# Moving the routing of an expert layer into the experts' block of a two-layer transformer kernel

## The reference

```python
scores = sigmoid(x @ w_gate.T)                          # [T, 16]
sv = scores.reshape(T, 4, 4)                            # 4 groups of 4 experts
group_scores = top_k(sv, 2)[0].sum(-1)
top_groups = top_k(group_scores, 2)[1]                  # 2 of 4 groups allowed
masked = where(allowed[:, :, None], sv, -inf).reshape(T, 16)
_, idx = top_k(masked, 4)                               # 4 experts of those
w = take_along_axis(scores, idx, 1); w = w / (w.sum(-1) + 1e-06)
combine = (one_hot(idx, 16) * w[..., None]).sum(1)      # [T, 16]
g = silu(einsum('th,efh->tef', x, w1_e)); u = einsum('th,efh->tef', x, w3_e)
routed = einsum('tef,ehf,te->th', g * u, w2_e, combine)
out = x + routed + swiglu(x, w1_s, w3_s, w2_s)
```

## Time and profile before

| | |
|---|---|
| median of 3 runs | 2229.55 us (2228.36, 2229.55, 2238.91) |
| the profiled execution | 2230.54 us, of which the span of the trace is 2228.7 us |
| TensorE busy | 1991.5 us, 89% of the span |
| VectorE busy | 1618.8 us, 73% |
| ScalarE busy | 1343.3 us, 60% |
| GpSimd busy | 1107.5 us, 50% |
| granted TensorE clock, mean | 0.95 of full |

### The profile page before, as it was taken

The page is one execution under the profiler, slowest core; times in us unless marked ns, Lnnn a source line. Parts: engine busy times, 40 slices in busy tenths (PEclk is TensorE's granted clock), DMA queues, the critical chain, the costliest instruction groups (busy, mean ns, idle before and its releaser), DMA issues. The chain is left out here.

```text
span 2228.7 us, 56143 instructions
## 1 busy us (share of the span) xinstructions
PE 1991.5 (89%) x17787; PEld 1012.5 (45%) x17787; DVE 1618.8 (73%) x3426; ACT 1343.3 (60%) x2148; POOL 1107.5 (50%) x994
## 2 busy tenths in 40 slices
PE   4788999999999999995599979999999999999775
PEld 3534444444444444445244424444444444444444
DVE  4977888888888888866677766566656666667896
ACT  2245666666666666663355547777877777778421
POOL 1432322222233222234254538777877778778565
PEclk7779999999999999997799979999999999999897
DMA  5621222112222211100012341111111111110000
GB/s 132 187 54 47 54 53 51 50 50 51 53 53 53 53 51 50 50 24 1 1 48 75 110 127 29 44 29 29 43 29 29 43 29 29 43 29 2 0 15 24
DMA packets 127064, 107.24 MB, mean 48 GB/s; under 512 B 39636, under 2 KB 102724, under 8 KB 126956
## 3 DMA queue, kind: packets, MB, share of 16 engines
q1 hardware_dynamic: 120544, 99.83, 16.9%
q10 hardware_dynamic: 6412, 6.18, 1.0%
HBM read 76.01 MB, written 29.53 MB: 47 GB/s over the span
## 5 line engine op out<-in xcount | busy, mean ns | idle before, releaser
L1103 DVE TENSOR_REDUCE b_mx<-psum 128x1 f32<-128x512 f32 x1024 | 664.0, 686 | 148.6 <-PE psum L920 83.4
L1087 ACT ACTIVATE b_prob<-psum 128x1024 f32<-128x1024 f32 x512 | 524.4, 1024 | 327.2 <-PE psum L952 327.1
L1917 POOL TENSOR_TENSOR combT<-attn,f_phi 128x512 f16<-128x512 f32 x512 | 587.0, 1157 | 182.0 <-ACT f_phi L2051 152.4
L2072 DVE TENSOR_REDUCE f_mx<-psum 128x1 f32<-128x512 f32 x512 | 328.6, 683 | 170.1 <-PE psum L1941 169.8
L2050 ACT ACTIVATE attn<-psum 128x512 f32<-128x512 f32 x512 | 308.0, 602 | 176.2 <-PE psum L1952 167.0
L1000 PE MATMUL psum<-b_prob,combT 128*32 128x256 f32 x4096 | 329.1, 393 | 1.5 <-ACT b_prob L1087 0.5
L852 POOL COPY combT<-v 128x64 f32 (+1 forms) x64 | 15.7, 246 | 604.4 <-PE psum L1000 594.8
L2051 ACT ACTIVATE f_phi<-psum 128x512 f16<-128x512 f32 x512 | 306.2, 598 | 0.0
L952 PE MATMUL psum<-x,b_toep 128*128 128x79 f16 (+1 forms) x4224 | 268.4, 208 | 0.0
L952 PEld LDWEIGHTS psum<-x,b_toep 128*128 128x128 f16 x4224 | 236.7, 99 | 9.3 <-issue 2.6
L855 POOL TENSOR_TENSOR x<-flip,grev 128x1024 f16<-128x1024 f16 x128 | 240.7, 1901 | 0.0
(11 more groups left out here) (321 smaller groups left out, 3391.4 us busy)
## 6 DMA issues: line engine op xcount, KB each, us to landing
f_qk<-d_qk SPq DMA_DIRECT2D x192, 128.0 KB, 2.9
d_qk<-e_qk SPq DMA_DIRECT2D x64, 256.0 KB, 2.6
b_toep<-d_line SPq DMA_DIRECT2D x128, 64.0 KB
b_q<-d_q SPq DMA_DIRECT2D x128, 54.0 KB
d_k<-a_qk SPq DMA_DIRECT2D x48, 128.0 KB, 2.3
b_toep<-d_line SPq DMA_DIRECT2D x128, 32.0 KB
b_q<-b_m SPq DMA_DIRECT2D x256, 1.0 KB
b_q<-d_q SPq DMA_DIRECT2D x128, 27.0 KB
```

The lines of the kernel that those rows point to most:

```text
L1087: nc.scalar.activation(prob[:, t % 4, :].rearrange("p (a n) -> p a n", a=2), ps[:, EXP + 2 * (t % 2):EXP + 2 * (t % 2) + 2, :], ACT.Exp).t ...
L1103: nc.vector.tensor_reduce(mx[:, b, t, half:half + 1], ps[:, bank, :], AX.X, ALU.max).then_inc(s.max_read, 1)
L1917: nc.gpsimd.tensor_tensor(plo[:, t % 4, at], prob[:, t % 4, at], phi[:, t % 4, at], ALU.subtract).then_inc(s.plo_ready, 1)
L2072: nc.vector.tensor_reduce(mx[:, b, t, half:half + 1], ps[:, bank + half, :], AX.X, ALU.max).then_inc(s.max_read, 1)
```

## The change

`phase_route` becomes `route_parts`, which has no block of its own: it hands out functions that `phase_experts` calls in its own block. Its scratch tiles lie in `g.attn` (free by then) and no longer in tiles of their own; the sizes are the same.

* VectorE: `choose` (the whole ranking for 32 tiles, and then the weights of the four tiles of chunk 0, `weigh(0, CT)`), the units 0 and 1 of chunk 0, then `weigh_rest` (the weights of the other 28 tiles), then the frames.
* TensorE: the turned weights; the GATE and UP products of units 0 and 1 without the COMB matmul; the four transposes of chunk 0 into bank 6; the two COMB matmuls; then frame 0, in which the four transposes of chunk 1 to 7 stand at the start of steps 2 to 8, all into bank 7. Frame 1 starts with a wait for the last of these to be moved.
* ScalarE: the moves of the turned weights; `silu` of unit 0; the move of chunk 0's shares; unit 1; in frame 0 the move of chunk c's shares stands ahead of unit c + 3 (for c = 6 and 7 ahead of the "next" units 0 and 1).
* GpSimd: the two clears of `g.combT`, then as before.

```diff
+    def choose(dve):
...
+        ranks(masked[:, :, :], rank[:, :, :], less16[:, :, :], cmp16, NE)
+        link(v.tensor_scalar(rank[:, :, :], rank[:, :, :], 3.5, None, ALU.is_lt))
+
+        def weigh(t0, t1):
+            sl, k = sc[:, t0:t1, :], t1 - t0
+            link(v.tensor_tensor(sl, sl, rank[:, t0:t1, :], ALU.mult))
+            link(v.tensor_reduce(total[:, t0:t1], sl, AX.X, ALU.add))
+            link(v.tensor_scalar(total[:, t0:t1], total[:, t0:t1], 1e-6, None, ALU.add))
+            link(v.reciprocal(total[:, t0:t1], total[:, t0:t1]))
+            link(v.tensor_tensor(sl, sl, total[:, t0:t1].rearrange("p (t a) -> p t a", a=1).to_broadcast([P, k, NE]), ALU.mult))
+            link(v.tensor_copy(hi16[:, t0:t1, :], sl))
+            v.tensor_copy(parts[:, t0:t1, 0:NE], hi16[:, t0:t1, :])
+            v.tensor_tensor(parts[:, t0:t1, NE:2 * NE], sl, hi16[:, t0:t1, :], ALU.subtract).then_inc(r.ready, 1)
+
+        weigh(0, CT)
+        r.weigh_rest = lambda: weigh(CT, NT)
...
+    def turn_shares(pe, c):
+
+        pe.wait_ge(r.ready, 1 if c == 0 else 2)
+        pe.wait_ge(r.moved, 1 if c == 0 else 1 + c)
+        for k in range(CT):
+            ins = nc.tensor.transpose(ps[0:2 * NE, bank_of(c), k * P:(k + 1) * P], parts[:, c * CT + k, :], g.ident[:, :])
+        ins.then_inc(r.turned, 1)
+
+    def move_shares(act, c):
+        act.wait_ge(r.turned, c + 1)
+        nc.scalar.copy(g.combT[0:2 * NE, c * CHUNK:(c + 1) * CHUNK], ps[0:2 * NE, bank_of(c), :]).then_inc(r.moved, 1)
...
+        routing.turn_weights(pe)
         for f in range(2):
-            up(0, 0, f)
+            up(0, 0, f, True)
+        routing.turn_shares(pe, 0)
+        pe.wait_ge(routing.moved, 2)
+        pe.wait_ge(routing.cleared, 2)
+        for f in range(2):
+            nc.tensor.matmul(ps[:, COMB + f, :], g.expert[:, f, :], g.combT[:, 0:CHUNK], start=True, stop=True).then_inc(s.up_psum, 1)
 
         def frame(n, u, units, ahead, out, projects, beside=None):
+            first = isinstance(n, int) and n == 0
+            if isinstance(n, int) and n == 1:
+                pe.wait_ge(routing.moved, NC + 1)
             for f in range(FT):
+                if first and 2 <= f <= NC:
+                    routing.turn_shares(pe, f - 1)
                 if f + 2 < FT and units:
                     up(n, u, f + 2)
...
-        for f in range(2):
-            unit(0, 0, f)
+        routing.move_weights(act)
+        silu(0, 0, 0)
+        routing.move_shares(act, 0)
+        unit(0, 0, 1)
 
         def frame(n, u, units, ahead, out, projects, beside=None):
             for kind, k in FRAME:
+                if isinstance(n, int) and n == 0:
+                    c = k - 3 if kind == "unit" else FT - 3 + k if kind == "next" else 0
+                    if 1 <= c < NC:
+                        routing.move_shares(act, c)
...
+        routing.choose(dve)
         for f in range(2):
             unit(0, 0, f)
+        routing.weigh_rest()
```

220 lines of the change are left out of this document (108 added, 112 removed).

## The result

The changed kernel took **2211.98 us** (median; 2208.41 to 2220.72), the kernel before 2225.78 us (2217.91 to 2270.44). Ratios leave out executions that are more than 1.5% above the fastest of their kernel; medians hold all. The ratio is 0.9941, with a 95% interval of [0.9922, 0.9961]: faster by 0.4 to 0.8%, some 13 us.

What follows compares the result with a forecast made beforehand. VectorE's ranking chain was taken to bound the path up to the first unit, TensorE from the second on. 8.9 us less 3.1 and 2.15 gave 3.65, so 2229.55 - 3.6 = 2225.9 us; range 2222 to 2231.

Steps and rivals of the forecast that it cites:

- The start: At the routing's barrier: seven `credit` increments ahead of VectorE's ranking delay it 0.5 us, bounds 0 and 0.9.
- Unit 0: First expert unit: VectorE starts it at about 1081.7 in place of 1090.56, 8.9 us earlier.
- The rest of the weights: Behind unit 1: VectorE's weights of the other 28 tiles take 3.9 us, nearly all covered by TensorE's own work.
- The clock: TensorE around frame 0's start: full clock back by 1088 or so, letting 17 matmuls end near 1089.5.
- Rival 3: Frame 0: half clock persists and makes the kernel slower, up to 18 us and 2244 us; chance 0.05.
- the late rise: Frame 0: full clock only at 1092, the 17 matmuls end at 1091.1, about 1.6 us longer, 2227.5 us.
- Waits: Frame 0: TensorE's turns wait for ScalarE's moves out of bank 7, which come in first, so no cost.
- Rival 2: Frame 0: bank 7 makes each turn wait 0.6 us, 3.6 us in all, no gain, 2229.5 us; chance 0.18.
- TensorE idle ahead of a turn: Frame 0: a gap before a chunk's transposes in the changed profile would show the forecast wrong; no size given.
- rival 1: Routing start and half clock of 1290.0 to 1293.3: more gain is kept, 2.5 us more, 2223.4 us; chance 0.12.
- The local sum: Routing through frame 0: 8.9 us won at unit 0, less 3.1 for VectorE's rest and 2.15 for transposes, 3.65 us.
- it carries to the end: Everything behind frame 0: shifts with it, so the whole 3.6 us comes off the total time.

Runs made afterwards that it cites:

- e4: Changed kernel with the split undone, all weights and all 32 transposes ahead of the first COMB matmul; ratio to the kernel before 0.9935.
- e7: Changed kernel with all of VectorE's weights ahead of unit 0, transposes still spread over frame 0; ratio to the kernel before 0.9924.
- e5: Kernel before with 252 ScalarE instructions more, waits long met, in the routing block; ratio 0.9963, second attention's loop 718.7 us.
- e6: Changed kernel with four ScalarE instructions more, waits long met, under the ranking; ratio to the kernel before 0.9971, second attention's loop 731.8 us.
- e1: Changed kernel run again with no edit; ratio to the kernel before 0.997, second attention's loop 717.8 us.
- e2: Kernel before run again as if a variant, with no edit; ratio 0.998, second attention's loop 726.8 us.
- e3: Kernel before with five TensorE instructions more, waits long met, at the routing block's end; ratio 0.9995, second attention's loop 728.5 us.
- e8: Changed kernel with 14 ScalarE instructions more, waits long met, under the ranking; ratio to the kernel before 0.9914, second attention's loop 709.8 us.
- e9: Changed kernel with the rest of VectorE's weights in three pieces, behind units 1, 3 and 5; ratio to the kernel before 0.995.
- e10: Kernel before with 10 ScalarE instructions more, waits long met, in the routing block; 2211.25 us beside 2235.44, ratio 0.9894.
- e11: Changed kernel without the split of VectorE's weights and with 14 ScalarE instructions more; ratio to the kernel before 0.9851, second attention's loop 709.3 us.
- e12: Kernel before with 216 ScalarE instructions more, waits long met; 2211.04 us beside 2222.81, ratio 0.9945, second attention's loop 709.1 us.

## Why the prediction was wrong, and where it was right

**The start.** Forecast 0.5 us for seven increments within 0 to 0.9; the ranking starts 0.65 us later behind the last score than before. Right, if all of it is the increments'.

**Under the ranking.** The 12 products and the turned weights ran from 1047.24 to 1053.7, all under VectorE's chain, as the forecast said: no cost.

**Weights of chunk 0.** Forecast 1.8 us, measured 1.75. **Unit 0.** Forecast 8.9 us earlier, measured 8.8.

**The rest of the weights.** Forecast 3.9 us (bounds 3.6 and 4.2), measured 4.6. This term was mis-sized: the first of its instructions, L1404 on 448 elements, took 1.13 us where L1411 of the same size took 0.62, beside GpSimd's `low` at 1075.13. The trace of before could not have shown it, since there the weights have GpSimd idle beside them.

**The clock.** Forecast back by 1088 in the time of before, which is 1079 here; it came back at about 1076.8.

```profile
1076.00:1077.00 1.00, 1.00 (x5) 0.33 (x4) 0.96 (x2) 0.38 (x1) 0.84 (x2) 0.60 0.00 0
1077.00:1078.00 1.00, 1.00 (x6) 0.48 (x5) 0.93 (x3) 0.00 (x0) 0.79 (x1) 1.00 0.00 0
```

Rival 3 is out, and so is the late rise. (The forecast read the second rise of the earlier trace rows at 1293.3; 0.55 in that window puts it at 1293.45. Nothing hangs on it.) The rule that the forecast set against itself (the Trainium skill, "TensorE: Matmul & The Clock Gate", Part 4: transposes don't count as TensorE being busy) is contradicted a second time, by e4, in which the clock rose at 1081.1 behind transposes alone.

**GATE of unit 5.** Forecast 5.8 us earlier, measured 5.7. **The other transposes.** 2.59 us per unit in place of 2.16, so 0.43 per chunk, as forecast. **Waits.** Forecast none for the moves, and there is none; ScalarE idles 0.69 us ahead of a move. Rival 2 is out. The two waits of 0.55 and 0.66 us for VectorE are the longer rest of the weights and its catching up; TensorE idle ahead of a turn was one of the forecast's own signs of being wrong, and the 0.55 us are that sign, small and with another cause than rival 2's. Of rival 1 nothing came either: `credit` and the weights of chunk 0 cost what was forecast, and the half clock of 1290.0 to 1293.3 is still there, 3.4 us long, from 1278.2.

**The local sum.** 3.65 us forecast, 3.5 measured. Here the mechanism and the sizes held. What the forecast did not see is how little of it is owed to the split of the weights (e7: none).

**The step that failed** is the one behind the sum: "Behind frame 0 everything hangs on it, so it carries to the end". The 3.5 us do carry to the end. But the sentence took the rest of the program to be the same work at the same time, since no line of it was edited. It is not: taking four instructions out of ScalarE's stream ahead of the second attention's loop moved its standstills off TensorE's path, 7.7 us (e5, e6). No rival had that mechanism, and nothing in the range stood for it. The second fault of the step: the sum was made against one execution, which held one event of 7.3 us; that belongs in the range, as do the 9 us by which the three times before already differed, of which the forecast took half a us. Part of the miss is no mechanism at all: the kernel before was 2229.55 us in the three executions that the forecast started from and 2225.78 in the twelve of the result, 3.8 of the 13.9 us between forecast and measured time. Of the gain itself, 13 us by the ratio and some 4 either way, 3.5 and 7.7 us are accounted for; the other 2 are within the interval.

How well the two parts, local and second loop, account for the measured ratios of all kernels. The gains are against the kernel before, 85.10 and 727.6 us; "ratio by it" is 1 less their sum / 2229:

```
               local   second   sum     ratio by it   measured [interval]
               gain    gain
after           3.5      7.7     11.2    0.9950        0.9941 [0.9922, 0.9961]
e1 (after)      3.5      9.8     13.3    0.9940        0.9970 [0.9926, 1.0013]
e2 (before)     0.0      0.8      0.8    0.9996        0.9980 [0.9944, 1.0017]
e3             -0.3     -0.9     -1.2    1.0005        0.9995 [0.9966, 1.0025]
e4              1.3      7.8      9.1    0.9959        0.9935 [0.9904, 0.9967]
e5             -0.2      8.9      8.7    0.9961        0.9963 [0.9924, 1.0002]
e6              3.5     -4.2     -0.7    1.0003        0.9971 [0.9932, 1.0011]
e7              3.4      8.4     11.8    0.9947        0.9924 [0.9889, 0.9959]
e8              3.5     17.8     21.3    0.9904        0.9914 [0.9875, 0.9952]
e9              1.5      8.2      9.7    0.9956        0.9950 [0.9904, 0.9996]
e10            -0.2     17.8     17.6    0.9921        0.9894 [0.9842, 0.9945]
e11             3.4     18.3     21.7    0.9903        0.9851 [0.9770, 0.9933]
e12            -0.2     18.5     18.3    0.9918        0.9945 [0.9896, 0.9995]
```

All thirteen ratios by this sum lie within the measured intervals, but these are 9 to 36 us wide: a weak test, and it is the traced stretches that carry the argument. By them the changed kernel is faster by some 11 us, of which about a third is the change's own and two thirds are the place of ScalarE's code. It has used up less than half of what that place is worth: e8's second loop is 10 us shorter still. The ratios, 0.9914 [0.9875, 0.9952] and 0.9941 [0.9922, 0.9961], don't tell the two apart.

**What is shown and what is argued.** Shown: moving ScalarE's stream alone, in either direction and in either kernel, sets the second loop's time (727, 719, 732, 710 and 709 us), and moving TensorE's by five doesn't. Shown too: which shifts cost (-4 and 0) and which don't (-40 and +10), and that each standstill at the return goes with a transfer of 8 KB of instructions, which the programs without standstills don't have there. Argued: that a piece is 128 instructions and that a store of four of them, with one fetched ahead, makes the difference. Open: what sets off the event in the first attention, why it brings nine packets, and whether a moved stream makes it rarer or more frequent. The two executions with most of them, e8 and e10, have a moved ScalarE stream, but so have e11 with two and e12 with none.

## What to carry to other kernels

A change also moves code: compare the stretches that the diff doesn't touch, and before half a per cent is put down to an idea, run the kernel before with some instructions of padding ahead of its long loops, engine by engine, and count the packets of the instruction queues on the page: 66 and 36 of q14 told the two cases apart here. Forecast the stretch, and put into the range what the loops behind it and the executions' own events can add. Where a change splits several things at once, test each alone: here the transposes were worth it, VectorE's weights weren't.

## What the runs showed of the hardware that was not expected

- ScalarE stood 1.6 to 1.9 us at a hardware loop's return and in some programs again 1 to 2 us later, with a transfer of 8 KB of instructions, depending on where the loop's 288 instructions lie. Six returns cost 0, 10, 18 or 23 us, by shifts of 4 to 40 instructions.
- At the return of TensorE's loop in the first attention 4.6 us pass at times without an instruction, with nine packets of 16 KB more over the pass, 5.4 to 7.7 us in all, by execution and not by program.
- Short VectorE instructions waited for GpSimd's two-input operation to end: one on 8 elements took 0.84 and 1.00 us where the same line on 12 took 0.17, one on 128 elements 0.8 us in place of 0.29.
- With seven semaphore increments ahead of it at a block's start VectorE's first instruction came 0.65 us later, some 0.09 us for each.
